# The first chunk's rank additions on GpSimd, half of the second chunk's products ahead of its selection

## What is computed

```python
def _sparsify_2to4(h):
    B, S, I = h.shape
    g = h.reshape(B, S, I // 4, 4)
    a = jnp.abs(g)
    _, idx = jax.lax.top_k(a, 2)
    pos = jnp.arange(4)
    mask = (pos == idx[..., 0:1]) | (pos == idx[..., 1:2])
    return (g * mask.astype(g.dtype)).reshape(B, S, I)
h = silu(x @ w_gate) * (x @ w_up)        # 256 x 1024 for one batch
return _sparsify_2to4(h) @ w_down        # added to x
```

## Time and profile before

| | |
|---|---|
| median of 3 runs | 433.79 us (431.8 to 436.32) |
| the profiled execution | 433.24 us, its span 431.5 us |
| granted TensorE clock, mean | 0.995 of full |
| chain that ended last, by engine | PE 66%, DVE 13%, issue 5%, ACT 5%, DMA 5%, POOL 4% |
| costliest lines in that chain | PE L550 13%, PE L425 11%, PE L614 9% |

### The profile page before, as it was taken

How to read it: one execution, slowest core, us unless ns; L and a number is a source line. 1 busy time by engine, 2 the same in 40 slices (tenths; PEclk the granted TensorE clock), 3 DMA queues, 4 the chain that set the end, 5 groups by cost and what they waited for, 6 DMA issues and landing times.

```text
span 431.5 us, 8030 instructions
## 1 busy us (share of the span) xinstructions
PE 396.5 (92%) x2978; PEld 321.7 (75%) x2978; DVE 284.9 (66%) x614; ACT 205.9 (48%) x530; POOL 160.0 (37%) x160
## 2 busy tenths in 40 slices
PE   8998999799899999889899999979899999988985
PEld 7666778676798777767698877757698877756873
DVE  5968832879779932788769951678769951345283
ACT  1374731677233731577334642287444452298320
POOL 4552870578301420378410430267520340066000
PEclk9999999999999999999999999999999999999998
DMA  7974422230001400240001400242000500310000
GB/s 222 373 277 144 136 82 73 76 92 2 2 2 64 139 26 24 75 124 18 2 0 47 155 2 2 73 117 52 0 2 2 168 28 2 98 51 2 0 2 24
DMA packets 34534, 29.95 MB, mean 69 GB/s; under 512 B 18752, under 2 KB 29120, under 8 KB 34240
## 3 DMA queue, kind: packets, MB, share of 16 engines
q1 hardware_dynamic: 34496, 29.44, 21.6%
HBM read 20.26 MB, written 5.24 MB: 59 GB/s over the span
## 4 chain that ended last, share of the span: by engine, by line
PE 66%; DVE 13%; issue 5%; ACT 5%; DMA 5%; POOL 4%; SPq 2%; POOLq 0%; DVEq 0%; ACTq 0%
PE ps L550 13%; PE ps L425 11%; PE ps L614 9%; PE ps L493 6%; PE ps L628 6%; PE ps L456 4%; DVE rope L781 3%; PE ps L433 3%; PE ps L514 3%; PE ps L536 3%; DMA q<-qx 2%; POOL prob L999 2%; DMA qx<-x_lo 2%; SPq L338 2%; DVE mx L809 2%
## 5 line engine op out<-in xcount | busy, mean ns | idle before, releaser
L999 POOL TENSOR_TENSOR prob<-prob,inv 128x512 f32<-128x512 f32 x80 | 83.0, 1043 | 106.1 <-DVE inv L829 106.0
L425 PE MATMUL ps<-xnT,wqk_sb 128*128 128x256 f32 x320 | 75.6, 383 | 0.7 <-DVE rope L781 0.4
L425 PEld LDWEIGHTS ps<-xnT,wqk_sb 128*128 128x128 f32 x320 | 58.7, 190 | 12.8 <-issue 5.5
L1105 ACT ACTIVATE prob<-ps,mx 128x128 f32<-128x128 f32 (+1 forms) x128 | 53.0, 435 | 14.2 <-DVE mx L807 11.1
L992 POOL TENSOR_TENSOR qs<-rope 128x512 f32<-128x512 f32 x32 | 40.8, 1276 | 35.1 <-DVE rope L781 32.4
L1115 ACT ACTIVATE pT<-ps 128x512 f32<-128x512 f32 x80 | 48.1, 605 | 11.7 <-PE ps L493 11.4
L493 PE MATMUL ps<-ident_sb,prob 128*128 128x128 f32 x320 | 48.9, 277 | 4.0 <-POOL prob L999 3.7
L781 DVE TENSOR_TENSOR rope<-ps,trig_sb 64x512 f32<-64x512 f32 x74 | 50.9, 688 | 1.0
L493 PEld LDWEIGHTS ps<-ident_sb,prob 128*128 128x128 f32 x320 | 37.0, 140 | 11.8 <-POOL prob L999 7.9
L978 POOL TENSOR_TENSOR rstd<-vareps,power 128x1 f32<-128x1 f32 x24 | 13.1, 551 | 82.0 <-DVE vareps L760 81.7
L807 DVE TENSOR_REDUCE mx<-ps 128x2 f32<-128x512 f32 (+1 forms) x48 | 33.0, 689 | 14.2 <-PE ps L475 13.8
(11 more groups left out here) (97 smaller groups left out, 704.3 us busy)
## 6 DMA issues: line engine op xcount, KB each, us to landing
k<-kx SPq DMA_DIRECT2D x32, 128.0 KB, 2.9
q<-qx SPq DMA_DIRECT2D x32, 128.0 KB, 2.5
vb<-v_sb SPq DMA_DIRECT2D x42, 64.0 KB, 2.1
wqk_sb<-in_wqk SPq DMA_DIRECT2D x4, 512.0 KB, 7.2
work<-in_wgu SPq DMA_DIRECT2D x4, 512.0 KB, 9.0
wo_sb<-in_wo SPq DMA_DIRECT2D x1, 2048.0 KB, 14.8
vb<-v_sb SPq DMA_DIRECT2D x36, 32.0 KB, 1.9
x_res<-in_x SPq DMA_DIRECT2D x4, 256.0 KB, 3.3
```

Source lines behind the costliest of these rows:

```text
L425: mm = pe.matmul(o[:, half, :], wqk_sb[:, k, g, half, :], xnT[:, 0, k, :], start=(k == 0), stop=(k == KT - 1))
L999: pool.tensor_tensor(p, p, inv[:, i % ND, 0:g].unsqueeze(2).broadcast_to([P, g, 512 // g]), ALU.mult).then_inc(s_norm, 1)
L1105: ins = act.activation(prob[:, i % ND, h * k:(h + 1) * k], ps[:, BANK_S + i % 2, h * k:(h + 1) * k], ACT.Exp, bias=mx[:, i % ND, h:h + 1], ...
```

## The change

The rank additions move into a helper `ranks(eng, b, c)`. In every batch, for chunk 0, it is called on GpSimd, at the end of GpSimd's batch; for chunk 1 it is still called on VectorE. `sparsify(b, 0)` on VectorE now ends with the comparisons. The selection becomes a function `select`, and VectorE runs the product `chunk_values(b, 1, 0)` before `select(b, 0)` and `chunk_values(b, 1, 1)` behind it. Nothing is computed differently, and no instruction is added or removed.

```diff
+        def ranks(eng, b, c):
+            n = FC * b + c + 1
+            eng.wait_ge(s_beats, n)
+            b01, b23, b02, b13, b03, b12 = (beats[:, k, :] for k in range(6))
+            eng.tensor_tensor(part[:, 0:2, :], beats[:, 2:4, :], beats[:, 4:6, :], ALU.add)
+            eng.tensor_tensor(part[:, 2, :], b02, b12, ALU.add)
+            eng.tensor_tensor(part[:, 3, :], b13, b03, ALU.add).then_inc(s_part, 1)
+            eng.wait_ge(s_part, n)
+            eng.tensor_tensor(wins[:, 0, :], part[:, 0, :], b01, ALU.add)
+            eng.tensor_tensor(wins[:, 1, :], part[:, 1, :], b01, ALU.subtract)
+            eng.tensor_tensor(wins[:, 2, :], b23, part[:, 2, :], ALU.subtract)
+            eng.tensor_tensor(wins[:, 3, :], part[:, 3, :], b23, ALU.add).then_inc(s_wins, 1)
...
                 dve.tensor_tensor(beats[:, 5, :], mag[:, 1, :], mag[:, 2, :], ALU.is_ge).then_inc(s_beats, 1)
...
-                dve.wait_ge(s_wins, n)
+                if c == 0:
+                    return
+                ranks(dve, b, c)
+                select(b, c)
+
+            def select(b, c):
+                dve.wait_ge(s_wins, FC * b + c + 1)
                 for j, (op, least) in enumerate(((ALU.is_ge, 2.0), (ALU.is_ge, 1.0), (ALU.is_ge, 0.0),
...
                 sparsify(b, 0)
-                for j in range(2):
-                    chunk_values(b, 1, j)
+                chunk_values(b, 1, 0)
+                select(b, 0)
+                chunk_values(b, 1, 1)
                 if more:
                     unit_max(b + 1, 0)
                 sparsify(b, 1)
...
                     next_group(b, "q7", 10)
+                ranks(pool, b, 0)
```

## The result

| | before | after |
|---|---|---|
| median of 4 timed runs each | 435.06 us | 448.02 us |
| ratio, 95% interval | 1 | 1.0269 (1.0221 to 1.0316) |
| profiled execution, time | 433.24 us | 446.99 us |
| profiled execution, span | 431.5 us | 445.2 us |
| granted TensorE clock, mean | 0.995 | 0.989 |

The change makes the kernel slower by 2.7%, 11.7 us on 435 (9.6 to 13.7). The ratio compares fast runs alone, while each median also counts one slow run (440.10 us before, 451.45 us after). The two profiled executions lie 13.75 us apart. The head of the page after shows the exchange that the change makes: DVE loses 7 us of work, POOL gains 20.

A forecast was written before the change was run, and what follows sets the result against it. The prediction took DVE's stream, with POOL's scaling behind it, to bound the hand-overs; three losses of 3.0 us plus 1.3 us in the last batch, 10.3 us on 433.24, gave 443.5 us, range 437.5 to 449.5.

The forecast's parts named there:

- the forecast's own band: Whole kernel, if the forecast holds (chance 0.59): 442.3 to 444.7 us, from 0.3 us either way per batch, four times.
- The sum: Three hand-overs at 3.0 us plus 1.3 us in the last batch: 10.3 us on 433.24, giving 443.5 us.
- a large fixed cost: Rival on POOL's additions: 0.55 us fixed each, loss 4.4 us per batch, 449.1 us; chance 0.10.
- clock drops at the hand-overs: Rival on PE: a 3.4 us half-speed stretch at each of three hand-overs adds 5 us, 448.6 us; chance 0.05.
- What bounds the hand-over: Feed-forward to next window stage: DVE's stream, then POOL's scaling, sets the pace; PE's transposes wait 0.59 us, full 3.0 arrives.
- only PE's lateness counts: Rival at the hand-overs: the window stage gives 1.1 us back, loss 1.9 us each, 440.2 us; chance 0.07.
- The allowance of 2.43 us: Chunk 0 of each batch: POOL's time for seven additions and the hand-overs before anything is lost.
- T: Time from chunk 0's last comparison's end to its selection's start, with the additions on POOL; taken as 5.4 us.
- a cheap bfloat16: Rival on POOL's additions: bfloat16 cheaper than float32, loss 0.7 to 1.3 us per batch, 436.0 to 438.4 us; chance 0.17.
- T = 3.8: Comparisons' end to selection by the skill's ratio of 1.96: about 3.8 us, loss 1.4 us per batch, 438.8 us.
- What hides PE's part: PE's two down-projections start 0.6 and 1.9 us later, with waits of about 0.6 and 1.3 us; PE partly covered.
- The clock in the last batch: Slow stretch moves into the first down-projection, hidden; last 16 matmuls take 3.69 us instead of 5.41, −1.7 us.

The follow-up runs named there:

- more cover: The change, but VectorE also runs both products of chunk 1 and the next batch's first maximum and subtraction before selecting chunk 0; ratio 1.0111 to the kernel before.
- the filled pair: The change and the kernel before, each with five filler matmuls in each of TensorE's two cross-attention pauses; medians 449.38 and 440.17 us.

## Why the prediction was right

The forecast was 443.5 us (437.5 to 449.5), slower; measured 448.0 us, slower. The mechanism holds, but the number does not speak for it by itself: the forecast's own band, 442.3 to 444.7, was missed by the median and by the profiled execution (447.0). The sum was 1.0 us too high in what it had and lacked 4.5 us beside it; the range held the result because it was drawn wide enough for the rivals. By the number alone the rivals of a large fixed cost (449.1) and of clock drops at the hand-overs (448.6) fit better; the traces rule both out. Step by step:

- **What bounds the hand-over.** Right. The transposes of the sixth window unit moved by 2.74 us per batch, by as much as the comparisons of chunk 1 (2.73), and PE waits 0.59 us there as before. The rival in which only PE's lateness counts (0.4 and 1.1 us at its two down-projections) is out.
- **The allowance of 2.43 us.** Right, in three settings: T of 5.16 lost 2.73, 3.54 lost 1.11, and with more cover the same 5.16 lost 0.80. With the same order and no work on POOL nothing was lost.
- **T.** Right in kind, 5% too large: 5.16 us instead of 5.4. The 128x256 additions took 0.67 us (0.69 said). The 128x512 one took 1.16 and not 1.285, so bfloat16 is a little cheaper than the float32 rows from which I took it, and no more. The two sizes give a fixed cost of 0.17 us. The rivals of a cheap bfloat16 and of a large fixed cost are both out, and so is T = 3.8, which the prediction got by taking the Trainium skill's float32 ratio of 1.96 ("GPSIMD Engine Reference", section "Elementwise — side-by-side cycle accounting") over to these additions. In bfloat16 the runs have 2.4 (0.67 against 0.28 us) and 2.7 (1.16 against 0.42); no run tests the float32 figure.
- **What hides PE's part.** PE waited 0.38 and 1.06 us at the down-projections (0.6 and 1.3 said, 3.0 − 2.73 = 0.3 less each).
- **The clock in the last batch.** Right: the slow stretch moved into the first down-projection, the last took 3.72 us, tail −1.67 (−1.7 said). With the pause filled the stretch was gone in either kernel, and in the change this gained nothing. That the kernel before had the stretch at all was taken as certain from one execution; in 10 of its 73 timed ones there was none, and there the change has no 1.7 us to give back. No clock below 1.00 stood around the first three hand-overs, so the rival of drops there is out.
- **The sum.** 3 × 3.0 + 1.3 = 10.3 was said, 3 × 2.73 + 1.06 = 9.25 holds. What was missing is cross-attention, which I had taken as moved but unchanged, from one execution: the waits for the queries' load, and the half-speed stretches that may stand behind them, made 4.5 us, 2.34 of them ahead of any changed instruction. That is why the profiled pair lies 13.75 us apart. On the filled pair the change costs 9.2 us; unfilled, it seems to cost a few tenths more per batch, with the cause not shown.

## What to carry to other kernels

Before moving work from a busy engine to an idle one, write down the allowance: the time that the work takes where it is, plus the work that can run in its shadow, and compare it with its time on the new engine with both hand-overs. A long idle time of the new engine says nothing of this, and work taken as cover must have its inputs by then. And ask which operands the two engines read at the same time: two engines that each read two operands from SBUF may take turns, so that a piece small enough to fit the allowance still costs more than it saves.

## What the hardware showed

- VectorE and GpSimd with two SBUF inputs each held one another up: a 128x256 bfloat16 addition on VectorE took 0.77 us beside GpSimd's and 0.28 us alone, GpSimd's 0.78 and 0.67 us.
- A GpSimd bfloat16 addition takes 0.67 us for 128x256 and 1.16 us for 128x512, against 0.28 and 0.42 on VectorE.
- A pause of TensorE of 1.75 to 2.8 us in cross-attention was followed by a stretch at half clock in some executions and not in others (1.91 us with and without one). One of 2.74 to 3.43 us in the last batch's down-projections was followed by one in all eight profiles that have it; one of 3.75 us was not.
- A float32 filler matmul of 128x256 takes 0.45 us (6 in 2.75 us), two records each.
